# Expert stage of a two-layer decoder: each group's store moved one group later in SP's order

## The reference, cut to what matters

```
C = ceil(1.5 * N / E)                                  # N = 8192 tokens, E = 8: C = 1536
buf = zeros(E, C, D).at[chosen_e, pos_c].add(x * kept)
h  = gelu(einsum('ecd,edf->ecf', buf, w1) + b1)        # D = 128, F = 512
eo = einsum('ecf,efd->ecd', h, w2) + b2
y  = eo[chosen_e, pos_c] * (chosen_p * kept)
```

## Time and profile before

| | us |
|---|---|
| median of 3 runs | 3335.85 |
| the profiled execution's own time | 3335.44 |
| its span, first to last instruction | 3333.7 |
| first to last matmul of the experts | 2032.37 to about 2273.2 |
| mean granted TensorE clock | 0.976 of full |

### The profile page before, as it was taken

The page is one execution under the profiler, slowest core; times in us unless marked ns, Lnnn a source line. Parts: engine busy times, 40 slices in busy tenths (PEclk is TensorE's granted clock), DMA queues, the critical chain, the costliest instruction groups (busy, mean ns, idle before and its releaser), DMA issues. The chain is left out here.

```text
span 3333.7 us, 98254 instructions
## 1 busy us (share of the span) xinstructions
PE 3019.8 (91%) x27585; PEld 2232.3 (67%) x27741; DVE 2417.5 (73%) x8136; ACT 2248.4 (67%) x8822; POOL 1391.3 (42%) x2572
## 2 busy tenths in 40 slices
PE   7999998999999999999999996777996999977777
PEld 4555555788888888888888874555664666654444
DVE  6888887677777777777777773114665899978886
ACT  6888887666666666666666663224774999975554
POOL 5777775122222222222222210004663777757775
PEclk9999999999999999999999998998997999989999
DMA  5000000100000000000000001221000000000000
GB/s 150 0 0 0 0 0 11 70 5 6 5 4 4 5 4 5 5 5 5 5 5 4 12 3 46 68 77 30 17 17 6 7 6 7 6 4 7 13 19 13
DMA packets 80374, 54.49 MB, mean 16 GB/s; under 512 B 24801, under 2 KB 74413, under 8 KB 80160
## 3 DMA queue, kind: packets, MB, share of 16 engines
q1 hardware_dynamic: 76192, 45.26, 4.8%
q0 software_dynamic: 4096, 8.16, 0.8%
HBM read 32.66 MB, written 20.97 MB: 16 GB/s over the span
## 5 line engine op out<-in xcount | busy, mean ns | idle before, releaser
L1100 DVE COPY b_prT<-b_tr 128x512 f32<-128x512 f32 x512 | 352.0, 687 | 237.8 <-PE b_tr L991 233.4
L1359 ACT ACTIVATE b_pr<-b_sc,b_low 128x205 f32<-128x205 f32 x1024 | 431.1, 431 | 33.9 <-DVE b_low L1076 33.9
L473 ACT ACTIVATE a_pr<-a_sc,a_low 128x128 f32<-128x128 f32 x1024 | 360.8, 387 | 11.7 <-DVE a_low L376 6.9
L1091 DVE TENSOR_SCALAR b_pn<-b_pr,b_rec 128x205 f32<-128x205 f32 x1024 | 298.5, 334 | 55.0 <-DVE b_rec L1085 0.3
L1417 POOL TENSOR_TENSOR b_ln_var<-b_ln_mean_var,all_eps 128x1 f32<-128x1 f32 x64 | 12.1, 189 | 757.8 <-DVE b_ln_mean_var L152 757.8
L991 PE MATMUL b_tr<-all_ident,b_pn 128*128 128x128 f32 x2048 | 323.0, 280 | 5.3 <-DVE b_prT L1100 3.1
L2149 ACT ACTIVATE f_pr<-f_sc,f_low 128x77 f32<-128x77 f32 x1024 | 316.0, 333 | 13.8 <-DVE f_low L2057 13.7
L512 POOL TENSOR_TENSOR a_pn<-a_pr,a_rec 128x512 f32<-128x512 f32 x256 | 261.2, 1042 | 123.1 <-DVE a_rec L384 106.8
L991 PEld LDWEIGHTS b_tr<-all_ident,b_pn 128*128 128x128 f32 x2048 | 227.0, 141 | 87.0 <-issue 79.2
L1076 DVE TENSOR_REDUCE b_low<-b_sc 128x4 f32<-128x820 f32 x256 | 256.2, 1001 | 9.3 <-PE b_sc L979 9.3
L979 PE MATMUL b_sc<-b_kT,b_q 64*128 64x205 f32 x2048 | 247.2, 359 | 0.0
(11 more groups left out here) (307 smaller groups left out, 8170.5 us busy)
## 6 DMA issues: line engine op xcount, KB each, us to landing
scratch_x<-b_zeros SPq DMA_DIRECT2D x12, 512.0 KB, 5.2
b_vm<-scratch_x SPq DMA_DIRECT2D x24, 256.0 KB, 3.0
scratch_y<-b_vt SPq DMA_DIRECT2D x24, 256.0 KB, 2.4
all_X<-in_x SPq DMA_DIRECT2D x8, 512.0 KB, 6.9
e_w<-in_e_w SPq DMA_DIRECT2D x16, 256.0 KB, 3.0
out_x<-all_X SPq DMA_DIRECT2D x8, 512.0 KB
w_mask<-in_mask SPq DMA_DIRECT2D x1, 2464.0 KB, 10.3
b_cT<-in_ctxT SPq DMA_DIRECT2D x32, 77.0 KB, 2.0
```

What stands on the lines that cost most here:

```text
L473: op = act.activation(pr[:, g, u], sc[:, g, 128 * u:128 * u + 128], ACT.Exp, bias=low[:, g, u:u + 1], scale=-1.0, accum_out=sums[:, g, u:u ...
L1091: op = dve.tensor_scalar(pn[:, j % 2, g, 0:KN], pr[:, j % 2, g, 0:KN], rec[:, j % 2, g:g + 1], None, ALU.mult)
L1100: dve.tensor_copy(prT[:, j % 2, i].rearrange("p h t q -> p (h t q)"), tr[:]).then_inc(prT_made, 1)
L1359: op = act.activation(pr[:, j % 2, g, 0:KN], sc[:, j % 2, h, KN * i:KN * i + KN], ACT.Exp, bias=low[:, j % 2, g:g + 1], scale=-1.0, accum_ ...
```

## The change

The store of a group stands behind the load three groups on, not two. In the first pair the store of group 0 so comes behind load 3, and one more store stands behind the loop over pairs.

```diff
@@ -620,14 +620,15 @@
                     if not due(n):
                         sp.wait_ge(scattered, 16 * B)
                     sp.dma_start(xr[:, k % 2], x_rows[n]).then_inc(x_loaded[k % 2], 16)
-                    if not (isinstance(j, int) and j == 0 and k < 2):
-                        store(n - 2, k % 2)
+                    if not (isinstance(j, int) and j == 0 and k < 3):
+                        store(n - 3, (k + 1) % 2)
 
         def store(n, ring):
             sp.wait_ge(y_done, n + 1)
             sp.dma_start(y_rows[n], yr[:, ring]).then_inc(stored[ring], 16)
 
         over_pairs(sp, body)
+        store(N * E // 2 - 3, 1)
         store(N * E // 2 - 2, 0)
         store(N * E // 2 - 1, 1)
```

## The result

The changed kernel takes 3283.35 us (median of 4 runs, 3281.56 to 3284.89) beside 3335.52 us of the kernel before (4 runs), a ratio of 0.9843 with a 95% interval of 0.9826 to 0.986. Five more runs later had a median of 3282.31. The prediction was 3283.8. The profiled execution took 3281.56, with a span of 3279.8.

The account below looks back on a forecast made before the run. It took the chain bias, store, load, transposes to bound the expert stretch. Gains of 4.98 + 5.25 + 41.85 = 52.08 us took the profiled 3335.44 to 3283.4, with the median 0.4 higher: 3283.8 us, range 3280.5 to 3292.

Parts of the forecast that it names:

- The chain that ends a step: Bias, store, load, transposes end each expert step, 0.9 to 1.3 us late inside an expert, about 4 at its start.
- A step of 7.45: Up to next up in the experts without any wait: 3.44 + 0.43 + 3.58 = 7.45 us.
- Step 2: From up(2) to the next up, with weight transposes: 12.75 us becomes 7.77, gain 4.98.
- Steps 3 and 4: Transposes here wait 1.22 us for ScalarE's copy, not the load: gain 0.
- Step 5: Load wait goes, ScalarE's last weight copy is late next: 14.12 us becomes 8.87, gain 5.25.
- Steps 6 to 22: The 17 later expert steps: 168.50 us becomes 17 x 7.45 = 126.65, gain 41.85.
- Edits at nothing: Moved weight loads, later-placed stores, SP arithmetic and the tail cost nothing; without cover, about 2 us in all.
- 3.1 us to spare at an expert's start: Row load at an expert's start: usable 7.8 us after up two groups earlier, wanted at 10.9.
- Rival 2: Load at an expert's start still late, six waits of 2 us, 12 us lost: 3295.8 us; chance 3%.
- Rival 3: Row load held by something other than the store, so the time stays at 3335.8 us; chance 2%.
- Rival 1: TensorE's clock doesn't come back entirely, seven downs stay slow, 11.3 us of gain lost: 3295.1 us; chance 5%.
- Rival 4: Slower: only 1.2 GHz granted in the 127 us of uninterrupted expert work, 3391.4 us; chance 1%.

Follow-up runs that it names:

- e1: Kernel before the change, with only the first row load of each expert asked for a group sooner: 3296.51 us, ratio 0.9879.
- e2: Kernel before the change, with only the row loads inside an expert asked for a group sooner: 3328.61 us, ratio 0.9977.
- e9: e2, with each expert's second row load also waiting until the transposes of its first group are done: 3323.49 us, ratio 0.9958.
- e6: Changed kernel, with the weight loads issued as late as before the change (those of expert 0 stay): 3282.00 us, ratio 0.9841.
- e7: Changed kernel, with ScalarE's copies of the last stage's transposed weights ahead of the group's GELU pieces: 3277.91 us.
- e4: Kernel before the change, with 24 extra identity transposes ahead of the row wait at groups 3, 6, 9 to 21: 3325.77 us, ratio 0.997.
- e3: Kernel before the change, with the row load at an expert's start issued ahead of the four weight loads: 3306.78 us, ratio 0.991.

## Why the prediction was right

- *The chain that ends a step* (bias, store, load, transposes). Right. e1 takes the long waits away and leaves the inner ones as they were; e2 and e9 take the inner ones away and leave the long ones. That the rows carry the gain and not the weights is shown by e6. The distance from store to load that the prediction gives as 0.58 "every time" is 0.43 to 0.61 in the trace; nothing hangs on it.
- *A step of 7.45.* 7.446 (126.58/17). The bounds of 1.7 and 1 us were not needed: from step 2 on every transposes that waits for nothing starts 3.43 to 3.44 after its up.
- *Step 2, 4.98.* 12.75 became 7.78: 4.97.
- *Steps 3 and 4, nothing.* 18.38 before, 18.37 after. That ScalarE's copy holds them is shown by e7.
- *Step 5, 5.25.* 14.12 became 8.89: 5.23. The wait that is late next, named ahead, is there with 1.25 us.
- *Steps 6 to 22, 41.85.* 168.50 became 126.58: 41.92. In all 52.13 for 52.08. The profiled run gained 53.88, because what lies behind up(23) was 2.3 us shorter and up(2) began 0.6 later: scatter. So the sum of the stretch was right by its terms, but that the median came within 0.5 us of 3283.8 is in part luck: its four runs spread over 3.3 us.
- *The slow work behind long waits* as part of the sum: right. e4 gives it back without moving a load. e2 and e9 show how loosely it follows the waits: with the inner waits gone, it grew by 2.6 and 3.9 us where it was expected to stay.
- *Edits at nothing.* Stores: VectorE waits for none. Weights: e6. The tail: from up(23) to the first matmul of the next stage is 16.9 us in both profiles (2262.41 to 2279.29; 2210.85 to 2227.77).
- *3.1 us to spare at an expert's start.* No wait appears, but the landing was taken too short for one of these loads: load 9 went out 6.98 us before its use and landed after 4.7 us, in both profiles of the changed kernel, where it had taken 3.8. So 2.3 us were to spare. The cause of this longer landing is open; the first loads of the other experts took 3.5 to 4.0, that of expert 1 at most 2.9. Rival 2, rows landing late in a burst, is thus a real mechanism, here in a dose that the spare time covered; a second row load beside the first is another (e2, e9). The changed kernel doesn't meet that one, because the store of group 3e-3 stands between loads 3e and 3e+1 and waits for its result: load 10 goes out 5.1 us behind load 9.
- *Rival 3.* The load was held by the store: with the store one group older it goes out a step sooner, and the time fell.
- *Rival 1 and the rule behind it.* Waits of 1.2 us leave the clock at 1.00, in the changed kernel (steps 3 to 5) and still more in e3, with 18 waits of 0.9 to 1.4 us in a stretch at 1.00. The case of short idle spells from the Trainium skill ("TensorE: Matmul & The Clock Gate", section "A second HAM failure mode: psum-queue depth-cycling") doesn't occur here; the measurement decides. The section before it, "HAM oscillation — how this bites in real kernels", describes waits for a DMA between tiles that leave each next tile slow; with this the trace agrees, in six of the seven long waits before the change.
- *Rival 4.* 50 us of TensorE without a pause, at 1.00.

## What to carry to other kernels

On a queue that issues loads and stores in order, look for what each load stands behind: a store that waits for the latest result makes every later load wait for it as well, and putting it one group later costs nothing if its own data is the last thing it waits for. Work out the gain from start to start of the bound engine's instructions, with the next-latest releaser of each step in its place, and include the work that ran slow behind long waits. Where several loads go out together, put the one that is wanted first ahead: that alone gave 29.8 us here (e3). When a load is moved forward, check that it doesn't go out beside the one that is wanted first.

## What was not expected of the hardware

The waits at an expert's start, 3.37 to 4.31 us before the change, left work that was slow for very different times: the down behind them took from 3.74 (behind 3.56 us) to 5.91 us (behind 3.87), and up to 6.12 in e9. Row loads of the same 256 KB landed in 2.8 to 3.2 us inside an expert, in 3.4 to 4.1 right behind the weights (before), and in 3.9 to 4.8 where two went out 0.6 us apart (e2).
